# Attention and expert kernel: LayerNorm statistics and weight pieces moved, a gate of 14 early tiles, and 95 unread TensorE products

## The chip, the cores and the metric

The kernel runs on one core of a Trainium2 chip. The metric is the device time of one launch in microseconds. A core has TensorE (PE, with its weight loads as PEld), VectorE (DVE), ScalarE (ACT), GpSimd (POOL) and SyncE (SP), each with a queue of its own that it works through in order, and 16 DMA engines.

## What is computed

Two sequences of 1024 tokens, 256 wide, go through cross attention with 16 heads over 64 context rows, and then through a mixture of 8 experts of which each token takes 2:

```python
x = x + xattn(layernorm(x), ctx, ctx, abundance, ...)     # softmax over 64 keys, plus log(abundance)
h = layernorm(x)
scores = softmax(h @ gate_w.T)
_, sel = top_k(scores + expert_bias, 2)
# tokens sorted by expert; for each expert e, on its own rows:
#   (silu(xe @ w1[e]) * (xe @ w3[e])) @ w2[e],  xe = h * score
x = x + sum over the two experts of a token
```

## The kernel before

**Tiling.** The 2048 tokens are T = 16 tiles of 128. The engines' programs are written out by hand, one block for each engine, with semaphores between them; what stands in a block is the order on that engine.

**First part (prologue).** The weights of the projections are transposed on PE, the keys are made, and the first two tiles get their LayerNorm and their queries. LayerNorm of the input needs, for each tile, `first_stats` (L825) and `first_moments` (L830) on DVE, `first_scales` (L471 to L477) on POOL for a group of tiles (`LN_GROUPS`: tiles 0 to 1, 2 to 3, 4 to 7, 8 to 15), and then `rows_apply` (on ACT, L643, for tiles 0 to 3; on POOL, L524, from tile 4).

**Attention steps.** A loop of 20 steps (`STEPS = T + 4`) is a pipeline: step t makes the scores of tile t on PE (L1258), their maximum and difference on DVE (L965, L984), in step t+1 the exponential on ACT (L734) and the transposes of the probabilities (PE L1342 in two halves, evicted by ACT L770), in t+2 the product with the values (PE L1286), its norm (DVE L974, L978), its transpose (PE L1313, ACT L744), the output projection (PE L1328, L1329) and the residual and second statistics (DVE L1023, L1027, L1031), in t+3 the second LayerNorm (POOL L539 to L545, ACT L756), and in t+4 its transpose (PE L1270, ACT L728) and the gate's logits (PE L1299, DVE L1016). The steps from 16 on have no new scores: this is the drain.

**Weight pieces.** The experts' weights are f32 in memory and are used as two f16 parts. They come in 32 pieces: kind 0 is 128x1408 (w1 or w3), kind 1 is 128x768 (half of w2). For each, SP issues a load into one of two stage buffers of its kind, ACT writes the high part (`piece_high`, L632) and POOL the low part (`piece_low`, L515). The table `plan` says which kinds each step takes, `late` which of the last expert's pieces, whose place in `w_hi` and `w_lo` holds the probabilities until then. SP issues the load two steps ahead and waits there until ACT and POOL are done with the buffer's previous piece.

**Gate.** For the first `EARLY` = 12 tiles the softmax, the comparison of experts (L943, L945), ranks (L950) and the choice (L951) run on DVE inside the steps 17 to 19; the other 4 tiles follow after the last step. Then PE counts (L1353 to L1364), DVE works out each token's slot and one-hot matrices (L1047 to L1073), PE makes the slots' tokens (L1370), and POOL gathers rows with `gather` (L571 a copy of the index column, L574 the indirect DMA).

**Experts.** J = 39 tiles of 128 slots: rows gathered, split into two f16 parts (ACT L784, DVE L1114), transposed by a DMA that SP issues (L418), w1 and w3 on PE (L1389 to L1391, 24 products of 352 columns a tile), SiLU and product (ACT L797, DVE L1126), split and transposed again (L435), w2 on PE (L1405 to L1408), and an indirect DMA that adds to the output (L605).

## Time and profile before

| | us |
|---|---|
| median of three runs (lowest to highest) | 438.52 (437.52 to 440.04) |
| the profiled execution | 439.58 |
| its span, first to last instruction | 437.8 |
| prologue and steps 0 to 2, until the first output transpose (L1313) | 0 to 47.0 |
| the steps up to the last tile's product with the values (L1286) | to 151.7 |
| the rest of the drain and the gate, until the slots' indices (L1091) | to 186.1 |
| until the first expert product (L1389) | to 194.1 |
| experts and the last copy | to 437.8 |

The profile page gives busy shares of the span in 40 slices of 10.9 us; a row PEclk gives the clock that TensorE was granted, in tenths of 2.4 GHz (5 is 1.2 GHz). A timeline row gives start, duration, engine, line, operation, output <- input, sizes, count, and in brackets how long the engine had been idle before it and what ended that.

### The profile page before, as it was taken

What the parts mean: (1) busy time and instruction counts of PE and PEld (TensorE: products, weight loads), DVE (VectorE), ACT (ScalarE), POOL (GpSimd) and SP (SyncE); (2) the same over time, 40 slices, a digit from 0 to 9 for tenths busy, and PEclk for the clock granted to TensorE, in tenths of its full rate; (3) what the DMA queues carried; (4) which work ended last, traced back from release to release, by engine and by line L of the source; (5) the groups of instructions that cost most, each with busy time, mean ns of one, the idle gap of its engine ahead of it and who ended that gap; (6) DMA issues with size and microseconds to landing.
All of it is one profiled execution on the core that took longest, in us unless ns stands there. A gap on an engine that the chain in (4) does not pass through costs nothing.

```text
span 437.8 us, 9846 instructions
## 1 busy us (share of the span) xinstructions
PE 354.1 (81%) x2573; PEld 266.7 (61%) x2574; DVE 240.5 (55%) x615; ACT 197.6 (45%) x343; POOL 237.0 (54%) x295
## 2 busy tenths in 40 slices
PE   2676699999888862128899999999999999999830
PEld 1455578888876752115567776767677767776620
DVE  1655776576665247925555555555555555555400
ACT  3567477787877632004333334333344444333300
POOL 6319786675775755041345565655555555664340
PEclk9886898898999655558999999999999999999995
DMA  7923676767895721023777777777777777889546
GB/s 235 317 26 96 187 213 162 198 184 162 241 214 167 238 60 20 0 73 64 122 125 135 136 138 136 135 134 135 133 134 134 135 138 130 133 136 143 95 57 204
DMA packets 121523, 61.53 MB, mean 141 GB/s; under 512 B 97170, under 2 KB 116124, under 8 KB 121468
## 3 DMA queue, kind: packets, MB, share of 16 engines
q1 hardware_dynamic: 113408, 50.45, 49.0%
q0 software_dynamic: 7488, 10.39, 15.6%
q10 hardware_dynamic: 604, 0.41, 0.4%
q8 instruction: 12, 0.20, 0.2%
q14 instruction: 11, 0.09, 0.1%
HBM read 28.88 MB, written 11.60 MB: 92 GB/s over the span
## 4 chain that ended last, share of the span: by engine, by line
PE 68%; DVE 10%; DMA 6%; ACT 6%; issue 4%; POOL 1%; SPq 0%; POOLq 0%; ACTq 0%; DVEq 0%
PE sc L1389 11%; PE sc L1390 10%; PE sc L1391 10%; PE bank L1286 6%; PE bank L1405 5%; PE bank L1408 5%; PE bank L1407 4%; PE bank L1328 3%; PE ptps L1342 3%; ACT w_lo L770 2%; DMA acc<-xn,put_now 2%; DMA arena<-x 2%; PE bank L1299 2%; PE ptps L1270 1%; DMA arena<-arena 1%
## 5 line engine op out<-in xcount | busy, mean ns | idle before, releaser
L1389 PE MATMUL sc<-w_hi,arena 128*128 x312 | 99.1, 318 | 11.8 <-DMA arena<-x 9.9
L605 POOL DMA_INDIRECT acc<-xn,put_now x39 | 62.5, 1601 | 74.4 <-DVE xn L1139 63.4
L1390 PE MATMUL sc<-w_hi,arena 128*128 x312 | 98.8, 317 | 0.0
L1391 PE MATMUL sc<-w_lo,arena 128*128 x312 | 98.7, 316 | 0.0
L797 ACT ACTIVATE arena<-sc,slot_score 128x352 f32<-128x352 f32 x78 | 43.2, 553 | 117.2 <-PE sc L1391 116.1
L1126 DVE SCALAR_TENSOR_TENSOR arena<-sc,slot_score,arena 128x352 f32<-128x352 f32 x78 | 45.5, 584 | 86.0 <-ACT arena L797 84.8
L515 POOL TENSOR_TENSOR w_lo<-stage_w,w_hi 128x1408 f16<-128x1408 f32 (+1 forms) x32 | 72.5, 2275 | 23.9 <-ACT w_hi L632 20.8
L1405 PE MATMUL bank<-w_hi,arena 128*128 x234 | 63.8, 273 | 3.8 <-DMA arena<-arena 2.0
L1408 PE MATMUL bank<-w_lo,arena 128*128 x234 | 61.7, 273 | 0.0
L574 POOL DMA_INDIRECT arena<-table,get_now x39 | 41.3, 1060 | 31.2 <-POOL get_now L571 31.2
L1407 PE MATMUL bank<-w_hi,arena 128*128 x195 | 53.2, 273 | 0.0
L1389 PEld LDWEIGHTS sc<-w_hi,arena 128*128 128x128 f16 x312 | 30.8, 99 | 34.8 <-issue 19.5
L1133 DVE TENSOR_TENSOR arena<-arena 128x64 f16<-128x64 f32 (+2 forms) x117 | 40.1, 398 | 10.1 <-ACT arena L804 9.6
L1391 PEld LDWEIGHTS sc<-w_lo,arena 128*128 128x128 f16 x312 | 30.9, 99 | 16.7
L571 POOL COPY get_now<-arena 128x1 int32 (+1 forms) x39 | 26.8, 688 | 26.1 <-DVE arena L1091 16.2
L1390 PEld LDWEIGHTS sc<-w_hi,arena 128*128 128x128 f16 x312 | 30.9, 99 | 14.5
L804 ACT ACTIVATE arena<-arena 128x704 f16<-128x704 f32 x39 | 30.8, 790 | 18.0 <-DVE arena L1126 18.0
L632 ACT ACTIVATE w_hi<-stage_w 128x1408 f16<-128x1408 f32 (+1 forms) x32 | 35.2, 1103 | 0.2
L1286 PE MATMUL bank<-v_blk,w_lo 128*128 128x34 f32 x256 | 32.2, 283 | 0.2 <-ACT w_lo L770 0.2
L1286 PEld LDWEIGHTS bank<-v_blk,w_lo 128*128 128x128 f32 x256 | 31.8, 202 | 0.8 <-ACT w_lo L770 0.7
L1405 PEld LDWEIGHTS bank<-w_hi,arena 128*128 128x128 f16 x234 | 22.9, 98 | 8.9 <-issue 4.7
L784 ACT ACTIVATE x<-arena 128x256 f16<-128x256 f32 x39 | 15.9, 407 | 22.7 <-DMA arena<-table,get_now 22.7
(187 smaller groups left out, 580.5 us busy)
## 6 DMA issues: line engine op xcount, KB each, us to landing
stage_w<-in_L_ffn_w SPq DMA_DIRECT2D x16, 704.0 KB, 4.7
stage_w<-in_L_ffn_w SPq DMA_DIRECT2D x8, 384.0 KB, 4.6
stage_w<-in_L_ffn_w SPq DMA_DIRECT2D x8, 256.0 KB, 2.6
acc<-arena SPq DMA_DIRECT2D x16, 128.0 KB, 1.8
table<-xn SPq DMA_DIRECT2D x16, 128.0 KB, 2.1
arena<-in_x SPq DMA_DIRECT2D x2, 768.0 KB, 8.2
stage_w<-in_L_ffn_w SPq DMA_DIRECT2D x16, 64.0 KB, 2.5
arena<-arena SPq DMA_TRANSPOSE x53, 5.2
```

Source lines behind the costliest of these rows:

```text
L515: pool.tensor_tensor(w_lo[:, cols], staged[:, :], w_hi[:, cols], ALU.subtract).then_inc(s["wlo"], 1)
L574: pool.indirect_dma_start(out=gx[par], out_offset=None, in_=table[:, :], in_offset=bass.IndirectOffsetOnAxis(ap=get_now[par][:, 0:1], axis ...
L605: pool.indirect_dma_start(out=acc[:, :], out_offset=bass.IndirectOffsetOnAxis(ap=put_now[par][:, 0:1], axis=0), in_=y_sb[par], in_offset=N ...
L797: act.activation(sil[par].rearrange("p (c n) -> p c n", c=2)[:, c, :], h1_ps[:, c, :], ACT.Silu, scale=slot_score[par][:, 0:1]).then_inc(s ...
L1126: dve.scalar_tensor_tensor(out=sil[par][:, cc], in0=h3_ps[:, c, :], scalar=slot_score[par][:, 0:1], in1=sil[par][:, cc], op0=ALU.mult, op1 ...
L1286: ins = pe.matmul(bk7[:, j * 2 * NOUT:(j + 1) * 2 * NOUT], probT[bt % 2][:, j * P:(j + 1) * P], v_blk[:, bt % 2, j, :], start=True, stop=True)
L1389: pe.matmul(ps[:, c, :], gT[par][:, k, :], w_hi[:, cols], start=k == 0, stop=False)
L1390: pe.matmul(ps[:, c, :], gT[par][:, KD + k, :], w_hi[:, cols], start=False, stop=False)
L1391: ins = pe.matmul(ps[:, c, :], gT[par][:, k, :], w_lo[:, cols], start=False, stop=k == KD - 1)
L1405: pe.matmul(bk7[:, 0:D], hT[par][:, c, :], w_hi[:, cols], start=c == 0, stop=False)
L1407: pe.matmul(bk7[:, 0:D], hT[par][:, KF + c, :], w_hi[:, cols], start=False, stop=False)
L1408: ins = pe.matmul(bk7[:, 0:D], hT[par][:, c, :], w_lo[:, cols], start=False, stop=c == KF - 1)
```

## The change

1. **Statistics.** On DVE the statistics of tiles 0 and 1 go behind the small operations on `cols3` and `ctxT`; those of tiles 2 and 3 ahead of the first `tokens_low`; those of tiles 4 to 7 ahead of `queries_low(1)` (they stood inside step 0); those of tiles 8 to 15, and the three operations on `bo16`, into step 0 (they stood in step 1). POOL's `first_scales` of the last group goes from step 2 to step 1. On ACT `queries_evict(0)` goes ahead of `rows_apply(2)`, and the high part of piece 0 into the middle of step 0.
2. **Pieces.** Steps 2, 3, 13, 14 and 15 take a piece of each kind; step 16 takes the last expert's two kind 0 pieces and step 17 its two kind 1 pieces, where they were spread over steps 16 to 19 (and POOL followed a step later). POOL now does three of these four low parts in step 17.
3. **Gate.** `EARLY` is 14: two tiles are left behind the last step.
4. **Waits.** The transpose of step t's second LayerNorm waits for one half of the probabilities' eviction less (`2 * min(t - 1, T) - 1`).
5. **Gathers** with a fixed tile number read their indices straight from `idx_get`, without the copy.
6. **Unread products.** `keep_clock(n)` issues n products of 512 columns (f16) on PE into `sc_ps[0]`, which nobody reads. There are 95: 31 in the steps 16 to 19 (1, 2, 2 in step 16; 2, 3, 2, 2 in step 17; 3, 2 in step 18; 10, 2 in step 19), 14 ahead of the wait for the choice, 24 ahead of the one-hot products, and 26 ahead of the wait for the experts.

The tables:

```diff
-        EARLY = T - 4
+        EARLY = T - 2
+        BEFORE_ROWS = [1, 2, 3, 10]
-        plan = [[], []] + [[0], [0, 1], [0], [1, 0], [1, 1]] * 3 + [[]] * 3
-        late = [[]] * T + [[0], [0], [1], [1]]
+        plan = [[], [], [0, 1], [0, 1], [0], [1, 0], [1, 1]] + [[0], [0, 1], [0], [1, 0], [1, 1]] + [[0]] + [[0, 1]] * 3 + [[]] * 4
+        late = [[]] * T + [[0, 0], [1, 1], [], []]
```

POOL's last pieces (in `step`) and `gather`:

```diff
+                if t == T:
+                    pool.wait_ge(s["o_ps"], T - 1)
+                    piece_low(LATE)
                 if t == T + 1:
                     pool.wait_ge(s["o_ps"], T)
-                for n in at_step[t]:
-                    piece_low(n)
-                if t > T:
-                    for n in late_step[t - 1]:
+                    for n in range(LATE + 1, len(PIECES)):
                         piece_low(n)
...
-                pool.tensor_copy(get_now[par][:, :], idx_get[:, col]).then_inc(s["get_idx"], 1)
-                pool.wait_ge(s["get_idx"], j + 1)
-                carry(pool)
+                if dyn:
+                    pool.tensor_copy(get_now[par][:, :], idx_get[:, col]).then_inc(s["get_idx"], 1)
+                    pool.wait_ge(s["get_idx"], j - 5)
+                    carry(pool)
+                    rows = get_now[par][:, 0:1]
+                else:
+                    rows = idx_get[:, col]
```

ACT in `step`, where `rows2_apply` is the second LayerNorm that stood there written out:

```diff
-                for n in at_step[t][0:1]:
+                if t > T and here(t, 3):
+                    rows2_apply(t - 3)
+                if late_step[t]:
+                    act.wait_ge(s["pt_ps"], 2 * (t - 1))
+                for n in (at_step[t] + late_step[t])[t == 0:1]:
                     piece_high(n)
+                if t == T + 1:
+                    for n in late_step[t][1:]:
+                        piece_high(n)
...
+                if t == T:
+                    piece_high(late_step[t][1])
```

PE:

```diff
+            def keep_clock(count):
+                for _ in range(count):
+                    pe.matmul(sc_ps[0][:, 0:512], ones16[:, :], shares16[:, None, :].broadcast_to([P, 4, P]), start=True, stop=True)
...
+                if t >= T:
+                    keep_clock(BEFORE_ROWS[t - T])
...
-                    pe.wait_ge(s["pt_sb"], 2 * min(t - 1, T))
+                    pe.wait_ge(s["pt_sb"], 2 * min(t - 1, T) - 1)
...
+            keep_clock(14)
             pe.wait_ge(s["selected"], 2)
...
+            keep_clock(24)
...
+            keep_clock(26)
             pe.wait_ge(s["experts_ready"], 1)
```

DVE in the kernel before, from the scores' maximum of tile 0 to that of tile 2 (L825 and L830 are the first LayerNorm's statistics, L1005 to L1008 the operations on `bo16`, L965 the maximum, L984 the difference, L862 `queries_low`, L855 `tokens_low`):

```order
L965 TENSOR_REDUCE top<-sc 128x16
...
L862 TENSOR_TENSOR arena<-bank,arena 128x8x32
L825 BN_STATS w_lo<-arena 128x6 x4
L830 BN_AGGR mv_all<-w_lo 128x2 x4
L965 TENSOR_REDUCE top<-sc 128x16
...
L825 BN_STATS w_lo<-arena 128x6 x8
L830 BN_AGGR mv_all<-w_lo 128x2 x8
L1005 CAST bo<-w_lo 128x256
L1006 SCALAR_TENSOR_TENSOR w_lo<-bo,low_rows,w_lo 128x256
L1008 CAST bo<-w_lo 128x256
L965 TENSOR_REDUCE top<-sc 128x16
```

DVE in the changed kernel, from the copy of `gateT` (L914) to the maximum of tile 2 (L836 and L841 are the statistics, L981 the maximum):

```order
L914 COPY gateT<-ptps 128x16
L836 BN_STATS w_lo<-arena 128x6 x4
L841 BN_AGGR mv_all<-w_lo 128x2 x4
...
L981 TENSOR_REDUCE top<-sc 128x16
...
L1005 CAST bo<-w_lo 128x256
L1006 SCALAR_TENSOR_TENSOR w_lo<-bo,low_rows,w_lo 128x256
L1008 CAST bo<-w_lo 128x256
L836 BN_STATS w_lo<-arena 128x6 x4
L873 TENSOR_TENSOR arena<-bank,arena 128x8x32
L836 BN_STATS w_lo<-arena 128x6 x4
L841 BN_AGGR mv_all<-w_lo 128x2 x8
L981 TENSOR_REDUCE top<-sc 128x16
```

The four statistics of tiles 4 to 7 have left the place between the maxima of tiles 0 and 1, and nothing of this kind stands any more between the maxima of tiles 1 and 2.

POOL in the drain before, from the second LayerNorm's scales of tile 14 (L539 to L545) to the first gather (L515 is a low part):

```order
L539 TENSOR_SCALAR ve<-mv 128x1
L543 TENSOR_TENSOR rs<-ve,neg_half 128x1
L545 TENSOR_SCALAR nmr<-mv,rs 128x1
L515 TENSOR_TENSOR w_lo<-stage_w_0,w_hi 128x1408
L539 TENSOR_SCALAR ve<-mv 128x1
L543 TENSOR_TENSOR rs<-ve,neg_half 128x1
L545 TENSOR_SCALAR nmr<-mv,rs 128x1
L515 TENSOR_TENSOR w_lo<-stage_w_1,w_hi 128x1408
L515 TENSOR_TENSOR w_lo<-stage_w_0,w_hi 128x768
L515 TENSOR_TENSOR w_lo<-stage_w_1,w_hi 128x768
L571 COPY get_now<-arena 128x1
L574 DMA arena<-table,get_now 128x264
```

The same stretch of POOL in the changed kernel:

```order
L540 TENSOR_SCALAR ve<-mv 128x1
L544 TENSOR_TENSOR rs<-ve,neg_half 128x1
L546 TENSOR_SCALAR nmr<-mv,rs 128x1
L516 TENSOR_TENSOR w_lo<-stage_w_1,w_hi 128x1408
L516 TENSOR_TENSOR w_lo<-stage_w_0,w_hi 128x768
L516 TENSOR_TENSOR w_lo<-stage_w_1,w_hi 128x768
L540 TENSOR_SCALAR ve<-mv 128x1
L544 TENSOR_TENSOR rs<-ve,neg_half 128x1
L546 TENSOR_SCALAR nmr<-mv,rs 128x1
L578 DMA arena<-table,arena 128x264 x6
```

The three last low parts stood behind the scales of tile 15 and stand ahead of them now.

PE in the changed kernel, from the start of step 17 to the count of the choices (L1244 is the unread product, L1289 the transpose of the second LayerNorm, L1307 the product with the values, L1322 the logits, L1338 and L1355 the output's transpose and projection):

```order
L1244 MATMUL sc<-shares,ones 128x512 x2
L1289 MATMUL ptps<-ident,xn 128x128 x2
L1244 MATMUL sc<-shares,ones 128x512 x3
L1307 MATMUL bank<-v_blk,w_lo 128x34 x8
L1322 MATMUL bank<-gateT,xn2T 128x8 x2
L1244 MATMUL sc<-shares,ones 128x512 x2
L1338 MATMUL bank<-ident,o_sb 128x128 x2
L1244 MATMUL sc<-shares,ones 128x512 x2
L1355 MATMUL bank<-woT,oT 128x256 x2
...
L1244 MATMUL sc<-shares,ones 128x512 x14
L1381 MATMUL bank<-sel,before_half 128x128
```

Without the rows of L1244 this is what stood there before.

## Rows read from the trace of the kernel before

**Rows 1.** The page: busy tenths and granted clock in 40 slices, the chain's shares.

```profile
PE   2676699999888862128899999999999999999830
...
PEclk9886898898999655558999999999999999999995
...
PE 68%; DVE 10%; DMA 6%; ACT 6%; issue 4%; POOL 1%; SPq 0%; POOLq 0%; ACTq 0%; DVEq 0%
```

**Rows 2.** Stretches: length, busy of PE, PEld, DVE, ACT, POOL, then granted clock.

```profile
150.00:160.00 10.00, 8.58 (x34) 6.77 (x32) 1.94 (x8) 4.27 (x6) 4.09 (x5) 0.50 0.21 66
...
300.00:400.00 100.00, 99.58 (x738) 70.61 (x737) 57.45 (x162) 39.63 (x72) 59.10 (x73) 1.00 0.78 136
```

**Rows 3.** Timeline (columns as told above) of steps 0 to 2.

```profile
20.24 0.42 DVE L862 TENSOR_TENSOR arena<-bank,arena 128x256 f16<-128x256 f32 x1 [2.68 <-ACT arena L659]
...
31.32 0.24 POOL L471 TENSOR_SCALAR ve_all<-mv_all 128x4 f32<-128x4 f32 x1 [10.85 <-DVE mv_all L830]
...
34.00 0.69 PE L1165 MATMUL bank<-ident,xn 128*128 128x128 f32 x2 [3.61 <-POOL xn L524]
34.46 4.46 POOL L515 TENSOR_TENSOR w_lo<-stage_w,w_hi 128x1408 f16<-128x1408 f32 x2
...
39.84 2.70 DVE L825 BATCH_NORM_STATS2 w_lo<-arena 128x6 f32<-128x256 f32 x8
...
44.80 1.22 DVE L965 TENSOR_REDUCE top<-sc 128x16 f32<-128x1024 f32 x1
...
47.02 0.69 PE L1313 MATMUL bank<-ident,o_sb 128*128 128x128 f32 x2 [3.90 <-DVE o_sb L978]
```

**Rows 4.** Timeline: the products with the values of tiles 13, 14 and 15.

```profile
136.65 1.94 PE L1286 MATMUL bank<-v_blk,w_lo 128*128 128x34 f32 x16
...
143.17 1.87 PE L1286 MATMUL bank<-v_blk,w_lo 128*128 128x34 f32 x16
...
151.68 3.47 PE L1286 MATMUL bank<-v_blk,w_lo 128*128 128x34 f32 x16
```

**Rows 5.** Timeline of the gate on DVE, beside POOL's last pieces.

```profile
159.88 0.26 DVE L925 TENSOR_TENSOR arena<-logits,arena 128x96 f32<-128x96 f32 x1
...
162.17 0.96 DVE L943 TENSOR_TENSOR arena<-arena 128x768 f32<-128x768 f32 x1
162.21 1.05 POOL L545 TENSOR_SCALAR nmr<-mv,rs 128x1 f32<-128x1 f32 x1
...
163.22 6.80 POOL L515 TENSOR_TENSOR w_lo<-stage_w,w_hi 128x1408 f16<-128x1408 f32 x3
...
165.21 1.68 DVE L951 TENSOR_SCALAR sel<-arena 128x96 f16<-128x96 f32 x1
...
167.23 1.25 DVE L925 TENSOR_TENSOR arena<-logits,arena 128x32 f32<-128x32 f32 x1
...
171.70 0.18 DVE L951 TENSOR_SCALAR sel<-arena 128x32 f16<-128x32 f32 x1
```

**Rows 6.** Timeline of PE's waits behind the gate, and POOL's first gather.

```profile
172.02 1.03 PE L1359 MATMUL bank<-sel,ones 128*128 128x120 f16 x15
...
182.58 0.72 PE L1370 MATMUL bank<-arena 128*128 128x39 f16 x16 [9.00 <-DVE arena L1073]
...
186.26 0.19 POOL L571 COPY get_now<-arena 128x1 int32<-128x1 int32 x1 [16.24 <-DVE arena L1091]
...
187.39 1.25 POOL L574 DMA_INDIRECT arena<-table,get_now  x1 [0.94 <-POOL get_now L571]
```

**Rows 7.** Timeline of the first expert tiles: PE's products of 352 columns of tiles 0, 1 and 2.

```profile
194.10 0.47 PE L1389 MATMUL sc<-w_hi,arena 128*128 x1 [8.60 <-DMA arena<-x]
...
199.93 0.36 PE L1391 MATMUL sc<-w_lo,arena 128*128 x1
...
202.22 0.31 PE L1391 MATMUL sc<-w_lo,arena 128*128 x1
...
205.43 0.32 PE L1389 MATMUL sc<-w_hi,arena 128*128 x1 [1.10 <-DMA arena<-x]
```

79 lines of the change are left out of this document (42 added, 37 removed).

## The prediction, made before the changed kernel ran

> **What bounds the kernel now.** I read the page's slices first. PE is at 9 tenths and more from slice 19 on, at the full clock of 2.4 GHz, and the chain lies on PE for 68% of the span [rows 1]. In the experts PE is busy for 99.58 of 100 us [rows 2]. Nothing in the change makes that part shorter, so a gain must come from the first 205 us. There the slices show two things: DVE, ACT and POOL with holes and peaks early on, and a clock row that falls to 5 (1.2 GHz) from slice 14 to 17, with PE at 8 in slice 14 and then at 1 and 2 [rows 1]. So in the drain PE is late and slow at once (8.58 of 10 us busy at 0.50 [rows 2]), in the gate PE waits for DVE, and the first expert tile starts at the low clock. The timeline then gives each place its price.
>
> **Statistics (part A).** At 34.00 PE transposes tile 4 after 3.61 us of waiting for POOL's `xn`, and POOL had sat idle for 10.85 us until DVE had the statistics of tiles 4 to 7 [rows 3]. In the changed order they come before `queries_low(1)`, where DVE was idle for 2.68 us; eight statistics took 2.70, so four take 1.35 and with their moments about 1.8: covered. The wait of 3.6 goes. What is late next is ACT, which evicts the values until about 31 and then has piece 1 ahead of tile 4, so I count 3.0. Second, from 39.84 to 44.80 DVE does eight statistics, moments and `bo16` ahead of the maximum of tile 2, while PE stands idle for 3.90 us up to 47.02 [rows 3]. These 4.96 us leave step 1. They come back in step 0, ahead of and behind `queries_low(3)`: 5.0 us against the 1.75 of tiles 4 to 7 that leave the place and a hole of about 2.7 us on DVE there; 0.5 us stick out. Together 3.0 + 5.0 - 0.5 = 7.5 us. The upper end is 9.5: tiles 2 and 3 get their scales about 1 us earlier too, and PE may keep its clock through steps 1 and 2. The lower end is 4: POOL has its two first pieces, 4.46 us [rows 3], still ahead of `rows_apply(6)`, SP waits for POOL before it loads into a used buffer, and step 2 now takes one low part more. I take 7.5, since POOL starts on piece 0 some 7 us earlier than at 34.46.
>
> **Drain and gate (part B).** The products with the values start at 136.65, 143.17 and 151.68 [rows 4]: 6.5 us a step at the full clock, 8.5 in the step in which it fell, and the last one takes 3.47 us where the others take 1.87. If the clock holds, 2.0 us go from step 16, 1.6 from the last product and about 1.4 from the transposes and projections behind it: 5.0. The unread products cost something where PE would not wait: the one at the head of step 16, the two behind its transposes, and the three ahead of the last product with the values, some 0.7 us. Then DVE. With POOL on the last three low parts for 6.80 us, the choice of 12 tiles took 1.68 us where the same operation on 4 tiles took 0.18 later, and the subtraction of 4 tiles took 1.25 where that of 12 took 0.26 [rows 5]. In the changed kernel these pieces are done before the late gate begins: 1.5 + 1.0 = 2.5, and 0.6 of a third such operation. The comparison and ranks of 2 tiles instead of 4 save another 0.6 (768 elements took 0.96 [rows 5]; three operations lose 128 elements each), less 0.2 on the early side. Against it stands the new order on POOL: three low parts, about 6.1 us, are ahead of the second LayerNorm's scales of tile 15, and the scales then meet DVE's comparison, as L545 did for 1.05 instead of 0.27 [rows 5]. I count 1.2 us for that. Behind the waiting POOL instruction stand ACT's normalization of tile 15, its transpose and its logits on PE, and the late gate. Sum: -5.0 + 0.7 - 3.1 - 0.4 + 1.2 = -6.6.
>
> The Trainium skill (SBUF — State Buffer, Who interferes with whom) says that VectorE and GpSimd share a port pair as an exclusive lock, and that a VectorE operation with two inputs in SBUF waits for a GpSimd operation that reads there. By that rule the three low parts of step 17 speak against the change, since they now lie beside the early gate's subtraction and scores; what that would make of the time is the second rival below. The rows agree with the lock as such: 1.25 and 0.26 us for the same operation [rows 5].
>
> **Counting and slots (part C).** 15 small products took 1.03 us at half clock [rows 6], with 16 smaller ones behind; at the full clock I take 0.6 us off. The one-hot products are hidden, DVE ends later.
>
> **Gather (part D).** The first gather started 1.13 us after the copy of its index did (0.19 for it and 0.94 idle [rows 6]). How much of the 0.94 is the indirect DMA's own preparation no row tells. At least the copy and a semaphore go, 0.3, at most 1.1. I take 0.5, nearer to the lower end, since in the timeline plain steps on POOL follow each other within some 0.1 us and most of the 0.94 is then the DMA's.
>
> **First expert tile (part E).** From 194.10 to 199.93, 20 products of 352 columns took 0.29 us each; from there to 202.22, 15 took 0.15 each [rows 7]. At the full clock from the start the first tile ends 2.8 us earlier. Tile 2 started at 205.43, released by its transpose [rows 7], which hangs on the rows' eviction behind tile 0's SiLU on ACT: it comes 2.8 us earlier too, so the gain is kept. -2.8.
>
> **The unread products behind the drain** take 512/352 x 0.15 = 0.22 us at the full clock, 0.42 at half. The 24 take 5.2 of a wait of 9.00 us [rows 6], the 26 take 5.7 of 8.60 [rows 7]; the 14 take 3.1 of about 3.5 behind the last logits. If the clock falls in the uncovered 3.8 us behind the 24, the 26 start slow; it then took 5.8 us of dense work to come back [rows 7], that is 14 of them, and the 12 others take 2.6: 8.4 of 8.1 us. So the experts start at the full clock at a cost of 0.3 at most.
>
> **Sum.** -7.5 - 6.6 - 0.6 - 0.5 - 2.8 = -18.0 from the profiled execution's 439.6 gives 421.6. That execution lies 1.1 above the median of the three runs, 438.5; steps 3 to 12 keep their pieces and I change nothing there. I forecast **421** us.
>
> **Rivals.**
> First, half of part A is eaten by POOL and SP: loads of steps 2 and 3 land late because two buffers wait for their low parts. For it: POOL was busy without a gap from 33.4 to 50. Against it: it starts 7 us earlier. Part A is then 4: 425.
> Second, by the port rule, the early gate is held up piece by piece: four operations of DVE with two inputs in SBUF (L925, L933, L937, L943), each by up to 1.0 us as L925 was, of which my sum has 1.2 for POOL's side. +3: 424.5.
> Third, the clock falls in the drain all the same, and only the 24 and 26 bring it back. Then 5.0 of part B and 0.6 of part C stay away, the 31 products in the steps take 0.42 us instead of 0.22, about half of them uncovered (+3), and the 14 take 5.9 of 3.5 us (+2.4): 421.6 + 11 = 432.6. For it: slices 13 and 14 show the fall with PE at 8 tenths [rows 1], so a busy PE alone did not prevent it. Against it: before it PE had waited behind ACT in each step, and the products are put into such waits.
> Fourth, **no gain, or slower**: the clock stays at half through the whole gate as well. Then part E goes (+2.8), the 24 end 1.1 us behind their wait, and the 26 2.3 us: 438.8. It is slower than before as soon as part A brings less than about 6.5 us; with 4 it is 442.
> The Trainium skill (TensorE: Matmul & The Clock Gate, Part 1) calls the slow clock the resting state, which activity lifts; by it the fourth case needs the dense 26 products to lift nothing, and [rows 7] show dense work lifting it.
> Fifth, more than the sum: the dips of the clock in slices 3 and 6 to 9 (6 to 8 tenths [rows 1]) go away with the stalls ahead of them; two to three steps at 3 us less on one of them and 1 us on the others: 417.
>
> **Chances.** Forecast (within 3 us) 0.46, first rival 0.15, second 0.12, third 0.12, fourth 0.05, fifth 0.10. The range from **414 to 431** takes in all but the third and fourth: 0.83. A measurement of this kernel can tell about 0.5% from no change, 2.2 us. Faster by more than that: all but the fourth and a small remainder, 0.93; within it 0.04; slower 0.03.
>
> **What would show it.** PE's wait ahead of tile 4's transpose under 1 us, and DVE's maximum of tile 2 near 38 instead of 44.80. Steps of 6.5 us up to the last product with the values, and that one at 1.9 us. The choice of 14 tiles at about 0.2 us. The clock row at 9 and more from slice 13 on, the first expert product near 176 and the 24 first ones at 0.15 us apart. The experts' part as long as before, about 232 us from tile 2 to the end. Wrong would be: PEclk at 5 in the drain with the unread products 0.42 us apart; POOL's scales of tile 15 more than 2 us behind the statistics; ACT waiting for weight loads in steps 2 to 4.

## The result

| | us |
|---|---|
| kernel before, median of the runs beside it | 438.79 |
| changed kernel, median (lowest to highest) | 414.82 (411.13 to 426.66) |
| ratio, with its 95% interval | 0.943 (0.935 to 0.950) |
| profiled execution, changed, and its span | 411.13, 409.4 |
| changed kernel run a second time (after_again): median, ratio | 414.61, 0.947 (0.940 to 0.953) |

The forecast was 421.0; the kernel gained 24 us, not 18. Runs that lie more than 1.5% above the fastest of their kernel count in the medians but not in the ratios: 426.66 here (without it the median is 413.89) and 425.77 in the second set, one run each of before_halfwait, after_pool_last, after_early12 and after_get_copy, three of the kernel before, and in before_fill and before_stats so many that no ratio is left.

The page of the changed kernel, the same rows as [rows 1]:

```profile
PE   2767999999999894889999999999999999999810
...
PEclk9896999999999996999999999999999999999985
...
PE 74%; DVE 8%; DMA 6%; issue 4%; ACT 3%; POOL 2%; POOLq 0%; SPq 0%; ACTq 0%; DVEq 0%
```

The clock row has lost its four slices at half speed in the gate; a 6 is left at slice 3, as before, and one at slice 15. In the gate PE is at 9, 4 and 8 (slices 14 to 16) where it was at 2, 1 and 2 (slices 15 to 17), but part of that is unread products. The chain lies on PE for 74% where it was 68%. Below are the drain, the stretch that answers the first of [rows 2], and the two places where the clock still falls:

```profile
32.00:36.00 4.00, 2.43 (x13) 1.71 (x12) 3.11 (x11) 1.57 (x3) 3.00 (x6) 0.50 0.63 164
...
132.00:142.00 10.00, 8.89 (x56) 5.83 (x55) 5.15 (x15) 4.80 (x9) 8.08 (x9) 1.00 0.17 57
158.00:162.00 4.00, 2.50 (x36) 1.57 (x36) 3.85 (x8) 0.00 (x0) 0.00 (x0) 0.50 0.01 4
```

The drain runs at 1.00, 2.4 GHz. The clock is at half (1.2 GHz) from about 31 to 37, after PE's idle time in step 1, and from 157 to 163, in and behind the longest wait that the unread products leave uncovered, the 3.80 us ahead of the one-hot products. The experts are as they were: from 280 to 380 us PE is busy for 99.49 us, at a granted clock of 1.00.

Where the time went, from milestone to milestone (each is the start of an instruction, in the two profiled executions; gain is the length before minus the length after):

| stretch | before | after | gain | forecast |
|---|---|---|---|---|
| start to tile 1's product with the values | 51.57 | 43.74 | 7.8 | 7.5 (A) |
| to tile 13's product | 85.08 | 75.97 | **9.1** | **0** |
| to the last choice (L951, L967) | 35.05 | 27.90 | 7.2 | 6.6 (B) |
| to the slots' indices (L1091, L1101) | 14.20 | 13.72 | 0.5 | 0.6 (C) |
| to the first expert product (L1389, L1419) | 8.20 | 7.76 | 0.4 | 0.5 (D) |
| to tile 2's first product | 11.33 | 8.41 | 2.9 | 2.8 (E) |
| to the end | 232.4 | 231.9 | 0.5 | 0 |
| sum | | | 28.4 | 18.0 |

Five of the six places up to tile 2's first product came out within 0.6 us of their term, and the rest of the experts within 0.5. The one that I left at nothing, twelve plain steps, brought 9.1. The profiled execution of the changed kernel is 3.7 below its median and had no fall of the clock in the twelve steps, so this sum flatters the change: by the medians 24 us are to be explained.

**Prologue.** Rows from the timeline of the changed kernel, answering [rows 3]; line numbers are its own (L981 maximum, L1005 and L1008 the two copies of `bo16`, L516 a low part, L1175 transpose of a tile of x, L1369 that of the probabilities, L1193 `queries`, L866 `tokens_low`):

```profile
25.06 2.85 POOL L516 TENSOR_TENSOR w_lo<-stage_w,w_hi 128x1408 f16<-128x1408 f32 x1 [1.10 <-ACT w_hi L635]
25.62 2.44 DVE L1005 CAST bo<-w_lo 128x256 f16<-128x256 f32 x1
...
28.47 0.39 PE L1175 MATMUL bank<-ident,xn 128*128 128x128 f32 x2
28.62 0.29 DVE L1008 CAST bo<-w_lo 128x256 f16<-128x256 f32 x1
31.36 1.11 PE L1369 MATMUL ptps<-ident,w_hi 128*128 128x128 f32 x4 [2.50 <-ACT w_hi L738]
...
34.04 0.39 PE L1193 MATMUL bank<-arena 128*128 128x256 f16 x1 [1.57 <-DVE arena L866]
37.67 1.23 DVE L981 TENSOR_REDUCE top<-sc 128x16 f32<-128x1024 f32 x1 [0.75 <-PE sc L1275]
40.46 0.44 PE L1338 MATMUL bank<-ident,o_sb 128*128 128x128 f32 x2 [0.34 <-DVE o_sb L994]
```

Tile 4's transpose starts at 28.47 without a wait (34.00 before, with 3.61), the maximum of tile 2 at 37.67 (44.80 before). What is late next is what the forecast had said, ACT: PE waits 2.50 us for the exponential of tile 0, and then 1.57 us for DVE's low part of a tile of x, behind the eight statistics that now stand in step 0. The wait ahead of the output's transpose is 0.34 instead of 3.90. Tile 0's product with the values comes 3.0 us earlier (40.68 to 37.68) and the step from it to tile 1's is 4.8 us shorter (10.89 to 6.06): the two halves of term A, 3.0 and 5.0 - 0.5. One cost stood in no term: the first copy of `bo16` on DVE now meets the low part of piece 0 on POOL, which ends at 27.91, and takes 2.44 us where the second, of the same size, takes 0.29. What these 2.15 us cost the kernel no run shows.

**Drain, gate, gather.** Rows of the same kernel from tile 13's product to the first expert product, answering [rows 4 to 7]:

```profile
119.71 1.97 PE L1307 MATMUL bank<-v_blk,w_lo 128*128 128x34 f32 x16
...
132.75 1.87 PE L1307 MATMUL bank<-v_blk,w_lo 128*128 128x34 f32 x16
...
134.70 6.09 POOL L516 TENSOR_TENSOR w_lo<-stage_w,w_hi 128x1408 f16<-128x1408 f32 x3 [0.91 <-PE bank L1307]
138.19 1.10 DVE L941 TENSOR_TENSOR arena<-logits,arena 128x112 f32<-128x112 f32 x1
...
142.64 0.60 ACT L775 ACTIVATE xn<-arena,nmr,rs 128x256 f32<-128x256 f32 x1 [2.75 <-POOL nmr L546]
144.83 0.22 DVE L967 TENSOR_SCALAR sel<-arena 128x112 f16<-128x112 f32 x1
...
147.61 0.17 DVE L967 TENSOR_SCALAR sel<-arena 128x16 f16<-128x16 f32 x1
147.91 0.65 PE L1387 MATMUL bank<-sel,ones 128*128 128x120 f16 x15
...
158.01 0.71 PE L1399 MATMUL bank<-arena 128*128 128x39 f16 x16 [3.80 <-DVE arena L1083]
...
161.33 0.18 DVE L1101 TENSOR_SCALAR arena<-arena 128x39 int32<-128x39 f32 x1
162.44 1.25 POOL L578 DMA_INDIRECT arena<-table,arena  x1 [19.84 <-DVE arena L1101]
163.99 0.96 POOL L578 DMA_INDIRECT arena<-table,arena  x1 [0.30 <-issue]
...
169.09 0.32 PE L1419 MATMUL sc<-w_hi,arena 128*128 x1 [1.14 <-DMA arena<-x]
```

The last two steps take 6.2 and 6.8 us, the last product 1.87 instead of 3.47, and the choice of 14 tiles 0.22 instead of 1.68 for 12. POOL's three low parts run from 134.70 to 140.79, and one operation of DVE meets them: the subtraction L941, 1.10 us, as [rows 5] had it for L925. The count takes 0.65 instead of 1.03, and PE's wait ahead of the one-hot products is 3.80 instead of 9.00. The gathers read their indices directly and follow each other with 0.30 us between them.

### The profile page after: what moved, and what is told of

Read it like the earlier page. It is cut to its first block, busy times and chain, and to the rows that moved or that the text cites. A ratio compares the mean times of both kernels' runs of the same rounds, so it can differ in the third digit from the quotient of the medians.

```text
span 409.4 us, 10006 instructions
## 1 busy us (share of the span) xinstructions
PE 358.7 (88%) x2668; PEld 263.6 (64%) x2669; DVE 239.3 (58%) x615; ACT 197.4 (48%) x343; POOL 234.8 (57%) x288
## 4 chain that ended last, share of the span: by engine, by line
PE 74%; DVE 8%; DMA 6%; issue 4%; ACT 3%; POOL 2%; POOLq 0%; SPq 0%; ACTq 0%; DVEq 0%
PE sc L1419 12%; PE sc L1421 11%; PE sc L1420 11%; PE bank L1307 7%; PE bank L1435 6%; PE bank L1438 6%; PE bank L1437 5%; PE bank L1355 3%; PE ptps L1369 3%; DMA acc<-xn,put_now 3%; DMA w_hi<-n_L_xattn_in_proj_weight 2%; PE bank L1322 2%; POOL w_lo L516 1%; PE sc L1244 1%; PE sc L1275 1%
## 5 line engine op out<-in xcount | busy, mean ns | idle before, releaser
L1419 PE MATMUL sc<-w_hi,arena 128*128 x312 | 97.8, 314 | 4.2 <-DMA arena<-x 2.2
L1421 PE MATMUL sc<-w_lo,arena 128*128 x312 | 97.6, 313 | 0.0
L1420 PE MATMUL sc<-w_hi,arena 128*128 x312 | 97.5, 313 | 0.0
L516 POOL TENSOR_TENSOR w_lo<-stage_w,w_hi 128x1408 f16<-128x1408 f32 (+1 forms) x32 | 71.7, 2255 | 13.4 <-ACT w_hi L635 12.3
L578 POOL DMA_INDIRECT arena<-table,get_now x32 | 34.4, 1075 | 25.6 <-POOL get_now L572 25.6
L1419 PEld LDWEIGHTS sc<-w_hi,arena 128*128 128x128 f16 x312 | 30.5, 98 | 27.1 <-issue 12.2
L1307 PE MATMUL bank<-v_blk,w_lo 128*128 128x34 f32 x256 | 31.4, 278 | 1.2 <-ACT w_lo L781 1.0
L1307 PEld LDWEIGHTS bank<-v_blk,w_lo 128*128 128x128 f32 x256 | 29.9, 192 | 3.8 <-ACT w_lo L781 3.3
L578 POOL DMA_INDIRECT arena<-table,arena x7 | 7.6, 1081 | 31.5 <-DVE arena L1101 19.8
```

The source lines that it names most:

```text
L516: pool.tensor_tensor(w_lo[:, cols], staged[:, :], w_hi[:, cols], ALU.subtract).then_inc(s["wlo"], 1)
L578: pool.indirect_dma_start(out=gx[par], out_offset=None, in_=table[:, :], in_offset=bass.IndirectOffsetOnAxis(ap=rows, axis=0)).then_inc(ga ...
L1307: ins = pe.matmul(bk7[:, j * 2 * NOUT:(j + 1) * 2 * NOUT], probT[bt % 2][:, j * P:(j + 1) * P], v_blk[:, bt % 2, j, :], start=True, stop=True)
L1419: pe.matmul(ps[:, c, :], gT[par][:, k, :], w_hi[:, cols], start=k == 0, stop=False)
L1420: pe.matmul(ps[:, c, :], gT[par][:, KD + k, :], w_hi[:, cols], start=False, stop=False)
L1421: ins = pe.matmul(ps[:, c, :], gT[par][:, k, :], w_lo[:, cols], start=False, stop=k == KD - 1)
```

## Experiments

The question is first where the 9.1 us of the steps come from. In this order: part 4 of the change alone and left out; fuller waits; part 1 alone; the unread products; the gate and the gathers. The piece plan (part 2) was not run by itself. Every ratio is against the kernel before, run beside it (440.0, 438.7 and 439.0 us in three sets). Where the intervals of two variants overlap, the times do not tell them apart, and only the stretches of their profiles, one execution each, are left to compare.

### Part 4, alone and left out

```diff
 # before_halfwait: the kernel before with part 4 alone (L1270 waits for one half less)
-                    pe.wait_ge(s["pt_sb"], 2 * min(t - 1, T))
+                    pe.wait_ge(s["pt_sb"], 2 * min(t - 1, T) - 1)
```

> The kernel before, with one edit: the transpose of the second LayerNorm waits for one half of the probabilities' eviction less. The steps were 6.45 us each and became 6.21 to 6.27; the dips of the clock in steps 6, 9 and 10 went too. Theory 1 (the shorter wait carries both): steps of 6.2 us and no dips, 9 us less than before, about 430. Theory 2 (the shorter wait gives 0.24 us a step, and the dips went for another reason): 3 us less, about 436, with the clock at half somewhere in the steps 4 to 12.

Measured: 428.4 us (428.4 to 436.0; before beside it 440.0, 434.1 to 440.5), ratio 0.979 (0.966 to 0.992). One changed number takes some 9 us off, with an interval of 3.5 to 15. That is the first theory's number, but not all of it is steps. Of the 11.2 us between the two profiled executions 7.7 lie in the twelve steps, in which one dip is left, 2.6 between tile 13's product and the choice, and 1.6 in the first expert tile, where the clock was back earlier; the experts behind it lose 1.0.

```diff
 # after_fullwait: the changed kernel without part 4
-                    pe.wait_ge(s["pt_sb"], 2 * min(t - 1, T) - 1)
+                    pe.wait_ge(s["pt_sb"], 2 * min(t - 1, T))
```

> The changed kernel, with the wait for the probabilities' eviction as it was before. Theory 1: the steps are 6.45 us again and the clock dips come back: 9 us more than the changed kernel, about 423. Theory 2: 3 us more, about 417, with the clock at full through the steps 4 to 12.

Measured: 422.2 us (420.2 to 423.1), ratio 0.964 (0.953 to 0.974); the interval lies above that of the changed kernel (0.935 to 0.950). It is the kernel that I had priced, and its time is 1.2 us from the forecast of 421, but in part by luck: in its profile the twelve steps gain 2.2 us where I had nothing, since the two dips of before are absent and a new one came from tile 12 to 13, and from tile 13's product to the choice it gains 3.4 instead of 6.6, with two fallen steps in it (8.12 and 8.63 us). The distances between the products with the values show the waits step by step (tile 1 to 2, 2 to 3, and so on to 13; a fallen clock in brackets):

| kernel | us |
|---|---|
| before | 6.83 6.69 7.27 [9.69] 6.68 6.74 [8.02] 7.27 6.51 6.45 6.45 6.48 |
| after_fullwait | 6.82 6.68 7.28 6.74 6.69 6.74 6.68 7.27 6.50 6.45 6.45 [8.58] |
| before_halfwait | 6.28 6.25 6.76 [7.70] 6.21 6.23 6.25 6.77 6.26 6.22 6.21 6.21 |
| after | 6.27 6.25 6.77 6.27 6.25 6.23 6.26 6.76 6.27 6.21 6.22 6.21 |

In this table undisturbed steps agree to 0.02 us between kernels with the same wait, and those with the half wait are 0.42 to 0.55 shorter up to tile 9 and 0.23 to 0.27 later. Over the first eleven steps that is 74.30 against 69.76 us (after_fullwait, after), and with the twelfth (6.48, taken from before, and 6.21) 4.8 in all. The rows show how. Timeline of the kernel before, at tile 12 (L1270 the transpose of the second LayerNorm, L770 ACT's eviction of the probabilities, L1286 the product with the values):

```profile
129.18 0.60 ACT L770 ACTIVATE w_lo<-ptps 128x512 f32<-128x512 f32 x1 [0.55 <-PE ptps L1342]
129.92 0.41 PE L1270 MATMUL ptps<-ident,xn 128*128 128x128 f32 x2 [0.33 <-ACT w_lo L770]
130.17 1.09 PE L1286 MATMUL bank<-v_blk,w_lo 128*128 128x34 f32 x9
```

and of the changed kernel, the same place at tile 11:

```profile
106.63 0.60 ACT L781 ACTIVATE w_lo<-ptps 128x512 f32<-128x512 f32 x1 [0.57 <-PE ptps L1369]
106.88 0.39 PE L1289 MATMUL ptps<-ident,xn 128*128 128x128 f32 x2
107.28 1.98 PE L1307 MATMUL bank<-v_blk,w_lo 128*128 128x34 f32 x16
```

Before, the transposes of 0.41 us wait until ACT has evicted the second half, and the product stands behind them. With the half wait they run during that eviction, and the product starts 0.65 us after the eviction's start instead of 0.99 (some 0.1 comes back in the product itself: 1.98 us for its 16 instructions, 1.87 before). The steps 4 to 11 gain twice as much because a second pair of transposes, of a tile of x (L1165), stands between the two and moves ahead with the first. The kernel before in step 11:

```profile
110.28 0.41 PE L1270 MATMUL ptps<-ident,xn 128*128 128x128 f32 x2 [0.92 <-ACT w_lo L770]
110.53 0.40 PE L1165 MATMUL bank<-ident,xn 128*128 128x128 f32 x2
110.76 1.87 PE L1286 MATMUL bank<-v_blk,w_lo 128*128 128x34 f32 x16
```

From the end of the wait to the product it is 0.48 us here and 0.25 at tile 12 (129.92 to 130.17). Eight steps with the one and four with the other make 4.8, which is what the steps gained. The length of the wait itself (0.33 to 0.92 us in these steps) does not set the gain: 0.92 gave 0.51 us and 0.33 gave 0.42 to 0.44.

The other part of the 9.1 are the bracketed steps. Windows of the kernel before over them:

```profile
76.00:84.00 8.00, 7.67 (x50) 6.56 (x48) 3.76 (x9) 5.27 (x10) 4.86 (x7) 0.71 0.65 182
96.00:104.00 8.00, 7.67 (x56) 6.76 (x54) 4.84 (x11) 5.43 (x11) 5.33 (x8) 0.79 0.91 207
```

The granted clock is 0.71 and 0.79 there on average, with PE busy for 7.67 of 8 us. 9.69 and 8.02 instead of 6.74 and 6.68 make 4.3 us, and 4.8 + 4.3 = 9.1. Do these dips go with the waits, or are they scattered? Counted between the products of tiles 1 and 14 over all profiled executions of this study, as steps more than 1 us over their usual length: with the full wait 2, 1, 3 and 2 (before, before_fill, before_stats, after_fullwait), with the half wait 1 in before_halfwait and 0, 1, 0, 1, 1, 2, 0, 0, 1 in the two profiles of the changed kernel and those of its seven variants below that have it. That is 2.0 against 0.7 a profile. It speaks for a link, and with it for the rest of part 4's worth: 7.4 us between the medians of after_fullwait and after, 4.8 of it the waits. With one profile a kernel it is not shown, and the 3 are those of before_stats, whose profiled run took 434.4 us where its fastest took 426.8. Behind this stretch, from tile 14 to 15, the clock fell in all four profiles with the full wait and in seven of the ten with the half one.

### Does a fuller PE keep its clock in the steps?

```diff
 # before_fill: the kernel before with one unread product in each of steps 4 to 15
                 if here(t, 4):
...
+                    if t < T:
+                        pe.wait_ge(s["ssub"], t)
+                        pe.matmul(sc_ps[(t - 1) % 2][:, 0:512], ones16[:, :], ...)
```

> The kernel before, with one unread product of 512 columns (0.22 us) on PE in each of the steps 4 to 15, ahead of the same wait, which stays as it was. It takes none of the wait away and only keeps PE busy in it. Theory 1a (the dips come from PE's idle time at this wait): the steps stay at 6.45 us, the dips go, about 6 us less, 433. Theory 2 (the dips have another cause): no difference within 1 us, or 1 to 2 us more, with the clock at half in steps 6 and 9 or 10 as before.

Measured: 435.3 us (429.5 to 436.8; before beside it 434.1 to 440.5), without a ratio. In its profile the step from tile 2 to 3 takes 8.03, and all others are as in the kernel before (6.82, 7.27, 6.75, 6.68 and so on): the product fits into the wait, costs nothing, and shortens no step; one dip is left where before had two, in a step that was filled, and the clock falls in the drain as before. The time lies between the two theories and decides nothing.

```diff
 # after_again: the changed kernel, unchanged, profiled a second time
```

> The changed kernel once more, as the measure for the three others of this group. Between 411 and 416, with steps of 6.2 us and at most one dip of the clock in them.

Measured: 414.6 us, ratio 0.947 (0.940 to 0.953). Its profiled execution has a span of 413.2, 3.8 more than the first one, and shows where they lie: 7.56 instead of 6.27 from tile 4 to 5, 8.19 instead of 6.83 from tile 14 to 15, and 1.0 in the experts. The page's clock row:

```profile
PEclk9996998999998998899999999999999999999985
```

The 8s in slices 6 and 12 are the two dips. So the dips have not gone with the change; they are fewer in some executions than in others, and the first profile was a lucky one. What PE did ahead of a dip does not tell the two apart. Windows of after_again over the first dip:

```profile
62.00:66.00 4.00, 3.61 (x34) 3.38 (x32) 2.91 (x8) 3.37 (x6) 3.10 (x3) 0.95 1.02 259
66.00:68.00 2.00, 2.00 (x12) 1.60 (x11) 1.05 (x1) 0.87 (x2) 1.90 (x4) 0.50 1.02 326
```

and of the first profile of the same kernel:

```profile
62.00:66.00 4.00, 3.62 (x34) 3.25 (x32) 2.95 (x7) 3.25 (x7) 3.26 (x3) 1.00 1.04 271
66.00:68.00 2.00, 2.00 (x14) 1.50 (x14) 1.31 (x2) 1.88 (x5) 1.90 (x4) 1.00 1.04 316
```

PE is busy for 3.61 and 3.62 of the 4 us, and the clock falls in one execution and not in the other.

```diff
 # after_fill_late: two unread products more in each of steps 12 to 15, ahead of the output projection
+                    elif t >= 12:
+                        pe.wait_ge(s["ssub"], t)
+                        for _ in range(2):
+                            pe.matmul(sc_ps[(t - 1) % 2][:, 0:512], ones16[:, :], ...)
```

> The changed kernel, with two more unread products of 512 columns in each of the steps 12 to 15, where PE waits 0.62 us for ACT ahead of the output projection. In these steps PE has no queries to make any more and is busy 1.4 of 2 us. If the clock dips that some executions have there come from this idle time, the runs above 415 go and the median falls by 2 us, to about 412; if not, it stays within 1 us of the changed kernel.

Measured: 413.8 us (411.4 to 416.6), ratio 0.944 (0.938 to 0.949). The interval overlaps both of the changed kernel, and the median did not fall by the 2 us of the theory. The two dips of its profile lie in the same steps as those of after_again, 7.56 and 8.19, the second of them behind the very products that should have kept the clock. The products cost 0.2 us in one step (6.40 instead of 6.21 from tile 11 to 12).

```diff
 # after_fill_pro: sixteen unread products in step 1
                 if here(t, 1):
+                    if t == 1:
+                        pe.wait_ge(s["ssub"], 1)
+                        keep_clock(10)
                     pe.wait_ge(s["p_exp"], t)
                     probs_over(t - 1, 0)
...
                 if here(t, -3):
+                    if t == 1:
+                        keep_clock(6)
                     queries(t + 3)
```

> The changed kernel with 16 unread products more, in step 1: ten ahead of the transposes of tile 0's probabilities, where PE of the changed kernel was idle from 28.9 to 31.4 us, and six ahead of queries(4), idle from 32.5 to 34.0. In the changed kernel the granted clock is 0.5 from 32 to 36 us, and the products of 256 columns from 34.04 on are 0.21 us apart instead of 0.11. Theory one: this dip, too, follows a wait, and a PE that works through the waits keeps its clock; then the work of PE from 34.04 to 39.5 us, about 5 us at half clock, takes 2 to 2.5 us less, of which ACT and DVE let 1 to 2 us through: tile 1's product with the values near 42.3 instead of 43.7, and 412 to 413 us in all. Theory two: PE isn't what is late in the prologue but ACT's and DVE's evictions: the clock row is at full, tile 1's product stays at 43.7 within 0.5 and the time at 414. Theory three: the dips of the steps come wherever PE has been busy for long: the clock falls at 30 to 40 us all the same, the six products then take 2.5 us where 1.5 are free, and the time is 414.5 to 416.

Measured: 414.8 us (413.6 to 417.0), ratio 0.946 (0.941 to 0.951). Windows of its profile:

```profile
30.00:38.00 8.00, 6.27 (x47) 4.23 (x45) 7.03 (x20) 6.16 (x11) 6.69 (x7) 1.00 0.52 148
38.00:40.00 2.00, 1.66 (x14) 1.36 (x14) 1.17 (x3) 1.81 (x2) 2.00 (x2) 0.97 0.21 30
40.00:42.00 2.00, 2.00 (x10) 1.57 (x8) 0.70 (x2) 1.07 (x3) 2.00 (x3) 0.50 0.90 319
```

The clock is held through 30 to 38 us, where it was at 0.50 for most of the time, and tile 0's product with the values comes 0.9 us earlier (36.78). Then the clock falls at 40 us, after ten in which PE had been busy for 7.9, and the step takes 7.66 instead of 6.06: tile 1's product comes at 44.44, 0.7 later than without the sixteen. The stall at 31 us was not what the dip needed; taking it away moved the dip. Three more steps of this profile dipped (7.53 from tile 9 to 10, 7.68 and 8.19 in the last two). This is a mixture of the first and third theory and no version to keep.

### Part 1 alone

```diff
 # before_stats: the kernel before with part 1 alone (core of it)
-                if t == 2:
+                if t == 1:
                     first_scales(*LN_GROUPS[3], 4)
...
+            for tt in range(*LN_GROUPS[2]):
+                first_stats(tt)
+            first_moments(*LN_GROUPS[2])
             queries_low(1)
```

> The kernel before, with part 1 of the change alone: statistics, scales, the operations on bo16 and piece 0's high part moved. Both theories: the product with the values of tile 1 starts 7.5 us earlier, at about 44. Theory 1: the dips stay and the time is 7.5 us less, about 431. Theory 2, in the form that the dips come from what the statistics hold up: they go as well, 13 us less, about 425.

Measured: 434.6 us (426.8 to 436.6), without a ratio. Its profile, of a run of 434.4 us, has tile 1's product at 43.66, 7.9 us earlier than before: term A is part 1 and needs nothing else. But in that execution the clock falls several times from tile 11 on and stays at half from about 130 us:

```profile
PEclk9997999999885555559999999999999999999985
```

Its last steps take 7.67, 7.92, 8.49 and 10.56 us where the kernel before had 6.45, 6.48, 6.52 and 8.51, and of the 7.9 only 5.5 are left at the last product with the values (146.15 against 151.68). What the statistics do to the dips it leaves open.

### The unread products

```diff
 # after_no_unread: no unread products at all
-                for _ in range(count):
+                for _ in range(0):
```

> The changed kernel without its 95 unread products. Theory 1 (they hold the clock up in the drain and bring it back for the experts): the last steps and the count at the half clock, 5 us, the first expert tile 2.9 us longer, less the 0.7 us that the products take: 7 us more than the changed kernel. Theory 2 (the denser steps alone keep the clock into the drain): the drain as in the changed kernel and only the first expert tile slower, 2 to 3 us more.

```diff
 # after_no31: the 31 of steps 16 to 19 left out, the 14, 24 and 26 kept
+            def keep_none(count):
+                pass
...
-                    keep_clock(BEFORE_ROWS[t - T])
+                    keep_none(BEFORE_ROWS[t - T])
... (and the same at the four other places in step)
```

> The changed kernel with the 14, 24 and 26 unread products, without the 31 in the steps 16 to 19. Theory 1: the clock falls in the drain (5 us more, less 0.7), the first expert tile stays at full clock: 4 us more than the changed kernel. Theory 2: no difference within 1 us.

Measured: 418.2 us without any (417.9 to 421.7), ratio 0.956 (0.950 to 0.963); 417.9 without the 31 (416.7 to 419.4), ratio 0.953 (0.947 to 0.959). Both intervals overlap those of the changed kernel (0.935 to 0.950 and 0.940 to 0.953), so by time the loss is likely and not shown; the profiles show where it lies. The clock rows of the two pages, after_no_unread and then after_no31:

```profile
PEclk9998999999996555599999999999999999999985
```

```profile
PEclk9896999999996568799999999999999999999985
```

| stretch | after | after_no_unread | after_no31 |
|---|---|---|---|
| tile 14's to tile 15's product | 6.83 | 7.69 | 7.92 |
| to the last choice | 14.86 | 18.68 | 18.69 |
| to the slots' indices | 13.72 | 14.19 | 14.94 |
| first expert product to the end | 240.3 | 242.4 | 239.8 |

Without the 31 the clock falls in slice 12, and the way from tile 15's product to the choice is 3.8 us longer in both kernels: this is what they hold. In all six profiles that have the 31 and the same gate and POOL order this way takes 14.86 or 14.87 us, also where the clock had dipped a step earlier. In after_no31 the 14 then start at the low clock (4.47 us from 151.33 instead of 3.18) and end behind the choice at 154.17, and the count starts 1.5 us behind the choice instead of 0.2. The 24 and 26 do lift the clock again, and the experts run at full speed from their first product; without them the experts are 2.1 us longer. In all the 95 products are worth 7.0 us between these two profiled executions and 3.6 between the medians (418.2 and 414.8). The two differ since the first profile of the changed kernel lies 3.7 us below its median, while that of the kernel without them lies on it; against the profile of after_again it is 3.2.

### POOL's order, the number of early tiles, the gathers

```diff
 # after_pool_last: POOL's last three low parts behind the scales of tile 15
-                if t == T + 1:
+                if t == T + 2:
                     pool.wait_ge(s["o_ps"], T)
```

> The changed kernel with POOL's last three low parts behind the second LayerNorm's scales of tile 15 (step 18), as in the kernel before, instead of ahead of them (step 17). In the changed kernel they run from 134.70 to 140.79 us, the comparison L941 of 14 tiles beside them takes 1.10 us, and the normalization of tile 15 starts at 142.64. Theory one, that of the prediction's terms: tile 15's scales come about 1.7 us earlier (0.8 of it from L941, 0.5 from the end of the pieces, 0.4 from L546), and the low parts then lie beside the late gate, whose operations with two inputs are held up as they were before, by 2 to 3.1 us in all. The choice is 0.3 to 1.4 us later than 15 us behind tile 15's product, and the time 414.3 to 415.5. Theory two: with two tiles in the late gate little of it falls beside POOL, the scales' gain stays: the choice comes about 1 us earlier, 412.8. In either case the low parts end near 147.5, more than 15 us ahead of the experts.

Measured: 416.1 us (414.2 to 421.8), ratio 0.948 (0.943 to 0.954); the choice comes 17.92 us behind tile 15's product instead of 14.86. Timeline of its gate:

```profile
138.21 0.27 DVE L941 TENSOR_TENSOR arena<-logits,arena 128x112 f32<-128x112 f32 x1
...
140.57 1.09 DVE L959 TENSOR_TENSOR arena<-arena 128x896 f32<-128x896 f32 x1
141.68 5.30 POOL L516 TENSOR_TENSOR w_lo<-stage_w,w_hi 128x1408 f16<-128x1408 f32 x2
141.70 3.77 DVE L961 TENSOR_TENSOR arena<-arena,tie 128x896 f32<-128x896 f32 x1
141.75 0.60 ACT L775 ACTIVATE xn<-arena,nmr,rs 128x256 f32<-128x256 f32 x1 [2.67 <-POOL nmr L546]
...
147.36 1.24 DVE L941 TENSOR_TENSOR arena<-logits,arena 128x16 f32<-128x16 f32 x1
```

The subtraction L941 of 14 tiles takes 0.27 (1.10 in the changed kernel) and tile 15's normalization starts at 141.75, 0.9 us earlier. Then the low parts meet the gate: L961 takes 3.77 us where it takes 1.09 in the changed kernel, as L959 of the same size does here, and L941 of two tiles takes 1.24 instead of 0.17. The loss is 3.1 us in this stretch, more than either theory allowed: they had 1.4 at most. The interval of the time overlaps that of the changed kernel.

```diff
 # after_early12: an early gate of 12 tiles
-        EARLY = T - 2
+        EARLY = T - 4
```

> The changed kernel with an early gate of 12 tiles instead of 14, all else as it is. The prediction priced the two tiles at 0.4 us (0.6 less on the late side, 0.2 more on the early side). Theory one: the choice comes 0.3 to 0.6 us later and the time is 414.3 to 414.6, the same within the measurement. Theory two: the late gate waits for something else that the number of tiles doesn't touch (the exponential on ACT, or a semaphore's way between engines), and the choice moves by less than 0.2 us. Theory three: the early gate's comparison of 14 tiles beside POOL's low parts holds up the residual of tile 15; with 12 tiles it is shorter by 0.1 us only, since the wait for the port and not the number of elements makes it long (1.10 us for 112 elements a partition).

Measured: 412.9 us (410.8 to 418.6), ratio 0.941 (0.933 to 0.950). The choice comes 15.07 us behind tile 15's product instead of 14.86, so the two tiles are worth 0.2 us, between the first theory and the second; L941 of 12 tiles takes 1.23 us beside POOL's low parts, no less than that of 14. By time the two kernels can't be told apart.

```diff
 # after_get_copy: the index copy ahead of every gather
-                if dyn:
+                if True:
                     pool.tensor_copy(get_now[par][:, :], idx_get[:, col]).then_inc(s["get_idx"], 1)
-                    pool.wait_ge(s["get_idx"], j - 5)
+                    pool.wait_ge(s["get_idx"], j + 1)
```

> The changed kernel with the copy of the index column and its semaphore restored ahead of every gather of a fixed tile, as in the kernel before. In the changed kernel the first gather starts 1.11 us behind the start of DVE's last operation on the slots' indices (161.33 to 162.44), in the kernel before it was 1.49 us (185.90 to 187.39), and the second gather follows the first one with 0.30 us between them. Theory one: the copy, its semaphore and its wait lie on the path to the first expert product: the first gather 0.3 to 0.5 us later, and the first expert product and the time with it, 414.2 to 414.5. Theory two: the first expert product hangs on the second gather or on the token's score as well, and the loss is twice as large, about 0.8 us, as the copy stands ahead of each. Theory three: it is hidden behind the other rows' way, and nothing moves.

Measured: 416.9 us (411.6 to 417.9), ratio 0.945 (0.935 to 0.955); the time says nothing, as its profile has two dips (7.68 and 10.93 in the last two steps). Its timeline says it:

```profile
166.33 0.18 DVE L1098 TENSOR_SCALAR arena<-arena 128x39 int32<-128x39 f32 x1
...
166.69 0.19 POOL L571 COPY get_now<-arena 128x1 int32<-128x1 int32 x1 [19.10 <-DVE arena L1098]
...
167.82 1.25 POOL L575 DMA_INDIRECT arena<-table,get_now  x1 [0.94 <-POOL get_now L571]
...
170.09 0.98 POOL L575 DMA_INDIRECT arena<-table,get_now  x1 [0.82 <-POOL get_now L571]
...
174.50 0.32 PE L1416 MATMUL sc<-w_hi,arena 128*128 x1 [0.85 <-DMA arena<-x]
```

The first gather starts 1.49 us behind the indices (1.11 in the changed kernel), the second 2.27 behind the first (1.55), and the first expert product 8.17 us behind the indices instead of 7.76: 0.4, the first theory's number. In the eight other profiles with the direct read this distance is 7.71 to 7.92, so 0.3 to 0.5; the second gather's delay of 0.7 is hidden.

## Why the prediction missed, step by step

**The step that failed** is the last sentence of the sum: "steps 3 to 12 keep their pieces and I change nothing there". The pieces are indeed the same, but part 4 of the change acts in every step from 4 on, and the prediction gives it no term at all. Without it the kernel takes 422.2, with it 414.8. The twelve steps brought 9.1 us between the two profiles: 4.8 by the wait of part 4, and 4.3 by two dips of the clock that this execution did not have. The wait stood in the timeline of before in each step ([0.33 <-ACT w_lo L770] on the transposes), and what stood behind it, 0.48 us of transposes in eight steps and 0.25 in four, gives the 4.8. Beside the rows of the drain [rows 4, 5] I should have read one plain step row by row, since any edit there counts twelve times.

**A**, 7.5: 7.8, and part 1 alone gives 7.9, with both halves near their terms. What was to be late next was: ACT, 2.50 us. The late loads of the first rival did not show: between 40 and 75 us ACT waited for PE alone.

**B**, 6.6: 7.2. Its terms came out less well than its sum. The clock with the unread products' own cost, 5.0 - 0.7 = 4.3: the kernel without them needs 4.7 more from tile 13's product to the choice. DVE and POOL, 3.1 - 1.2 = 1.9: the reversed order costs 3.1. The two tiles, 0.4: 0.2. Added up that is 8.0 against the measured 7.2, in which there are also 0.3 of part 4 (6.52 to 6.21 from tile 13 to 14): each was measured as the loss when it alone is undone, and such losses need not add up. The Trainium skill (SBUF — State Buffer, Who interferes with whom) says that a DVE operation with two inputs in SBUF contends with a POOL operation that reads SBUF; the trace agrees, with L941 at 1.10 us beside a low part and 0.27 without one, and L961 at 3.77 and 1.09. The second rival put 3 us on the early gate for it. The order decided instead: one operation met the low parts (0.8 us), as they were done before the rest with two inputs began.

**C, D, E**: 0.6, 0.5 and 2.8 against 0.5, 0.4 and 2.9. D was the term with the widest bounds; the choice near the lower end was right.

**The third and fourth rival** (the clock falls in the drain all the same, or stays low through the gate) did not come. In after_no31 the fall cost less than the third rival had written for it: its span is 7.3 us longer, with a dip of 1.4 from tile 13 to 14 in it, and by medians 3.1, where the rival's parts without the 31 products were 8.0. The rival's argument misread the page by one slice: PE is at 8 tenths in slice 13 and at 6 in slice 14, where the clock is at half. In every kernel here that had them, the 24 and 26 left the experts at the full clock.

**The fifth rival**, dips that go away, is half true. They were absent in the first profile, and present, smaller, in the second. The one cause that was put forward, stalls ahead of them, found no support: filling the waits (before_fill, after_fill_late, after_fill_pro) left or moved them. A cause is not shown by any run here; what is shown is that they come in steps ahead of which PE had been busy for 7.9 of 10 us (after_fill_pro) or 3.61 of 4 (after_again), that the same 4 us passed without one in another execution, and that they cost 1.3 to 3 us each in the twelve steps, at places that vary with the kernel and the execution. Of the miss of 6.2 us between forecast and median 4.8 are the waits of part 4; the remaining 1.4 is no more than one dip or the small errors of the other terms, and stays open.

The range of 414 to 431 was too narrow below: the median of 414.8 lies at its edge, and that of the three runs from 411.1 to 415.8 (413.9) just outside. It was made of rivals for the terms that I had, and none of them could pay for a term that was missing.

## What to carry to other kernels

A wait that stands in a loop's body is priced by the work that it holds back times the trips, however small it is: one number in a semaphore's wait took 4.8 us off these steps, and 7 to 9 by the medians, as much as the whole prologue. Unread products held or restored TensorE's clock across the waits of the drain and the gate, worth 3.8 us on the way to the choice and 2.1 in the experts by the profiles and 3.6 by the medians, and did not stop dips in a busy stretch. And put GpSimd's long operations on SBUF where VectorE has little to do there: the same three operations cost it 0.8 us at one place and 3.7 at another, and a copy with one input can be held up as well as an operation with two (2.44 us instead of 0.29).

## What the runs showed of the hardware

- A DVE operation of two SBUF inputs beside a POOL operation is not slowed by a factor, the rows show it waiting for the end of the POOL operation that ran when it began: 0.27 us became 1.10 (112 elements), 0.17 became 1.24 (16 elements), 1.09 became 3.77 (896 elements). In after_pool_last L961 started at 141.70, POOL's low part ran from 141.68 to 144.53, and L961 ended at 145.47; L941 ended at 148.60, the low part beside it at 148.57.
- The same holds for some DVE operations with one SBUF input: the copy L1005 took 2.44 us and ended at 28.06, 0.15 us behind a low part, while L1008 of the same size took 0.29; in the kernel before the choice L951 took 1.68 us and ended 0.07 us behind a low part (166.90 and 166.83), where it takes 0.22 in the changed kernel.
- TensorE's granted clock can fall to half in the middle of busy steps and come back although the steps go on as before: in after_again it is 0.50 from 66 to 68 us, behind 4 us with PE busy for 3.61, while in another execution of the same kernel it stays at 1.00 behind 4 us with PE busy for 3.62; in after_fill_pro it is 0.50 from 40 to 42 us.
- Undisturbed steps repeat to 0.02 us between kernels with the same wait, so a difference of 0.2 us a step can be read from one profile, while single executions of one kernel scatter by 5 us (411.13 to 415.76, 413.37 to 418.67).
- Two indirect gathers in a row that read their indices directly stand 0.30 us apart; with a copy ahead of each there are 0.94 and 0.82 us between a copy and its DMA alone.
